# When the expert weights of a graph layer are loaded, and where rows of other experts are masked

## The reference, cut to what matters

```
xn = layernorm(x)                                         # x: 3125 x 256
x  = x + relational_gnn(xn, src, dst, edge_type)          # 50000 edges, 8 relations, 4 bases
       + linear_attention(xn)
xf = layernorm(x)
idx = argmax(xf @ router_w.T + router_b, axis=-1)         # 32 experts, one for each row
h   = relu(xf @ W1[idx] + b1[idx])                        # 256 -> 64
out = relu(h @ W2[idx] + b2[idx])                         # 64 -> 256
x   = x + out
```

## Time and profile before

| | |
|---|---|
| median of 3 runs | 611.94 us (611.05 to 613.35) |
| profiled execution, its own time | 615.56 us |
| its span in the trace | 613.7 us |
| PE, DVE, POOL busy | 86%, 67%, 69% of the span |

### The profile page before, as it was taken

The page is one execution under the profiler, slowest core; times in us unless marked ns, Lnnn a source line. Parts: engine busy times, 40 slices in busy tenths (PEclk is TensorE's granted clock), DMA queues, the critical chain, the costliest instruction groups (busy, mean ns, idle before and its releaser), DMA issues.

```text
span 613.7 us, 10819 instructions
## 1 busy us (share of the span) xinstructions
PE 530.2 (86%) x3165; PEld 445.4 (73%) x3165; DVE 410.6 (67%) x1510; ACT 213.8 (35%) x435; POOL 423.4 (69%) x447
## 2 busy tenths in 40 slices
PE   0656889999968899999999999999996888999880
PEld 0556889999857778888888878888875775776650
DVE  6899587777654647767666676767565870878741
ACT  6685633321107112424243343424240005652300
POOL 6777777777777677777777777777777777334313
PEclk9978899999978699999999999999996658999795
DMA  8994333333354334445454545445448767451101
GB/s 274 266 263 145 104 108 109 104 104 105 110 162 132 99 107 130 141 143 151 138 159 130 154 135 159 141 146 155 135 141 247 216 171 209 134 182 61 45 28 40
DMA packets 47976, 87.17 MB, mean 142 GB/s; under 512 B 11059, under 2 KB 29524, under 8 KB 47784
## 3 DMA queue, kind: packets, MB, share of 16 engines
q0 software_dynamic: 21872, 60.77, 34.1%
q1 hardware_dynamic: 25032, 24.99, 12.9%
q10 hardware_dynamic: 1008, 0.65, 0.4%
HBM read 73.68 MB, written 12.70 MB: 141 GB/s over the span
## 4 chain that ended last, share of the span: by engine, by line
PE 63%; DVE 14%; DMA 7%; POOL 6%; issue 6%; ACT 1%; DVEq 1%; ACTq 0%; POOLq 0%
PE ps L1027 25%; PE ps L1098 12%; PE ps L1081 6%; DMA gath<-xn_d,src_i 6%; POOL gath L682 4%; PE ps L1047 3%; PE ps L1354 3%; PE ps L1069 3%; PE ps L1363 3%; DVE both L2044 2%; POOL acc_raw L682 2%; DVE raw_stats L1501 1%; DMA rel_of<-in_relation_of 1%; PE ps L1323 1%; DVE acc_raw L1590 1%
## 5 line engine op out<-in xcount | busy, mean ns | idle before, releaser
L682 POOL DMA_INDIRECT gath<-xn_d,src_i x263 | 250.6, 953 | 83.4 <-issue 68.6
L1027 PEld LDWEIGHTS ps<-wmat,gath 128*128 128x128 f32 x1052 | 153.3, 213 | 39.3 <-issue 20.6
L1027 PE MATMUL ps<-wmat,gath 128*128 128x80 f32 (+1 forms) x1052 | 161.6, 303 | 15.3 <-DMA gath<-xn_d,src_i 15.1
L682 POOL DMA_INDIRECT acc_raw<-xn_d,src_i x96 | 91.0, 948 | 29.2 <-issue 24.1
L1590 DVE TENSOR_TENSOR acc_raw<-acc_raw,ps 128x144 f32 (+1 forms) x392 | 88.4, 266 | 27.9 <-PE ps L1027 17.9
L1563 DVE TENSOR_TENSOR ps<-rel,iota 128x144 f32<-128x144 f32 (+1 forms) x98 | 28.1, 286 | 92.0 <-PE ps L1027 90.9
L1027 PE MATMUL ps<-wmat,acc_raw 128*128 128x144 f32 x512 | 71.4, 294 | 9.2 <-ACT acc_raw L790 7.8
L1027 PEld LDWEIGHTS ps<-wmat,acc_raw 128*128 128x128 f32 x512 | 68.7, 195 | 12.3 <-issue 8.8
L1567 DVE TENSOR_TENSOR wmat<-ps,wts 128x576 f32<-128x576 f32 (+1 forms) x98 | 62.0, 632 | 3.4
L731 POOL DMA_INDIRECT out<-both,out_i x24 | 24.7, 1030 | 46.2 <-DVE both L2044 22.7
L1098 PE MATMUL ps<-wk_et,acc_raw 128*128 128x256 f32 (+1 forms) x200 | 53.7, 394 | 0.6 <-DVE acc_raw L1590 0.6
(11 more groups left out here) (289 smaller groups left out, 757.2 us busy)
## 6 DMA issues: line engine op xcount, KB each, us to landing
rows_d<-both SPq DMA_DIRECT2D x24, 256.0 KB, 2.5
gath<-xn_d,src_i POOLq DMA_INDIRECT x263, 2.8
both<-in_x SPq DMA_DIRECT2D x24, 128.0 KB, 3.4
both<-in_x SPq DMA_DIRECT2D x4, 640.0 KB, 10.4
xn_d<-both SPq DMA_DIRECT2D x4, 640.0 KB
acc_raw<-in_w_t SPq DMA_DIRECT2D x8, 260.0 KB
acc_raw<-in_w_t SPq DMA_DIRECT2D x8, 256.0 KB
acc_raw<-xn_d,src_i POOLq DMA_INDIRECT x96, 2.8
```

Source lines behind the costliest of these rows:

```text
L682: g.indirect_dma_start(place_of(n), None, table, bass.IndirectOffsetOnAxis(ap=src_i[:, n:n + 1], axis=0)).then_inc(done, 16)
L1027: ins = t_.matmul(ps_edge[quarter][:, m * w:(m + 1) * w], place_of(n)[:, m * P:(m + 1) * P], wmat_tiles[:, k, 0:w], start=k == pair[0], st ...
```

## The change

Weights: expert e's segment of `acc_raw` lies in a quarter of the tiles (e modulo 4). The 16 transfers of weights keep their size, but each takes four experts of one quarter, and it is issued after a row store and an x load of the chain: after tiles 4 to 7, 12 to 15 and 17 to 20 one each, the last four around the stores of tiles 22 and 23. The small transfers follow tile 10. No transfer waits for edge matmuls any more.

Mask: one matmul for each group (bf16, 512 columns) first writes 0 or -3e38 into the PSUM bank of the hidden layer, and the W1 products add to it. ReLU covers 65 rows instead of 64; the 65th has bias 1, so it gives 1 for own rows and 0 for others. DVE builds the mask `never` in `find_pairs` and two small tables in `count_below`. `limit`, the eight memsets of ones and the buffer `picked` go. DVE does a pair in one operation, max with 0 and add to the rows; each waits for the one before.

```diff
-        def load_experts(c):
-            nc.sync.wait_ge(c.pre_done, NS)
...
-            for i in range(PIECES):
-                a, b = X // PIECES * i, X // PIECES * (i + 1)
-                if c is once:
-                    nc.sync.wait_ge(multiplied, OCT * (BRANCH + 1) + OCT // 2 * i)
-                nc.sync.dma_start(segs[:, a:b, 0:P], of_w1[:, a:b, :]).then_inc(ffn_loaded, 16)
-                nc.sync.dma_start(segs[0:H + 1, a:b, W2_AT:W2_AT + D], of_w2[:, a:b, :]).then_inc(ffn_loaded, 16)
+W_LOADS = {**{4 + i: (0, i) for i in range(4)}, **{12 + i: (1, i) for i in range(4)}, **{17 + i: (2, i) for i in range(4)}}
+        def load_piece(eng, quarter, i):
+            half = X // 2 * (i // 2) + quarter
+            of = slice(half, half + X // 2 - 3, 4)
+            if i % 2 == 0:
+                eng.dma_start(segs[:, of, 0:P], of_w1[:, of, :]).then_inc(ffn_loaded, 16)
+            else:
+                eng.dma_start(segs[0:H + 1, of, W2_AT:W2_AT + D], of_w2[:, of, :]).then_inc(ffn_loaded, 16)
...
                 load_x(sp, t + 3, once)
+                if t in W_LOADS:
+                    load_piece(sp, *W_LOADS[t])
+                elif t == SMALL_LOADS:
+                    load_small(sp)
...
+                    bank = ps[5 + g % 2]
+                    t_.matmul(bank[0:H + 1, :], groups[:, g:g + 1].to_broadcast([NPAIR, H + 1]), never.rearrange("p f n -> p (f n)"),
+                              start=True, stop=True)
...
-                            pe.wait_ge(f_read, FT * (g - 2) + f // 2 * 2 + 2)
+                            pe.wait_ge(f_y, FT * (g - 2) + f // 2 * 2 + 2)
...
+                at = o.mark(d.tensor_scalar(member, iota[0:NPAIR, :], facts[0:NPAIR, 2:3], None, ALU.is_ge))
+                at = o.mark(d.scalar_tensor_tensor(member, iota[0:NPAIR, :], facts[0:NPAIR, 3:4], member, ALU.is_lt, ALU.mult))
+                o.mark(d.scalar_tensor_tensor(never, member.unsqueeze(1).to_broadcast([NPAIR, FT, P]), 1.0,
+                                              of_four.unsqueeze(2).to_broadcast([NPAIR, FT, P]), ALU.subtract, ALU.mult))
...
-                        d.tensor_scalar(picked(f), ps[g % 2 * 2 + f // 2][:, f % 2 * D:(f % 2 + 1) * D], limit[:, p:p + 1], 0.0,
-                                        ALU.min, ALU.max).then_inc(f_read, 1)
-                        if f % 2 == 1:
-                            for j in range(2):
-                                place = token_flat[:, ds(tiles[f - 1 + j] * ROW + D, D)]
-                                d.tensor_tensor(place, place, picked(f - 1 + j), ALU.add).then_inc(f_y, 1)
+                        if p > 0:
+                            v.wait_ge(f_y, p)
+                        place = token_flat[:, ds(tiles[f] * ROW + D, D)]
+                        d.scalar_tensor_tensor(place, ps[g % 2 * 2 + f // 2][:, f % 2 * D:(f % 2 + 1) * D], 0.0, place,
+                                               ALU.max, ALU.add).then_inc(f_y, 1)
```

More of the change, by code:

```diff
@@ L442, in gps_layer @@
         at = 0
[L443 to L448, removed]
+        spread = e_flat[:, at:at + 2 * NPAIR].rearrange("p (c j) -> p c j", j=NPAIR)
+        at += 2 * NPAIR
+        never = e_flat[0:NPAIR, at:at + FT * P // 2].bitcast(BF16).rearrange("p (f n) -> p f n", f=FT)
+        at += FT * P // 2
+        member = blank[0:NPAIR, :]
+        of_four = bv_bc[0:NPAIR, 6 * X:6 * X + FT]
+        groups = bv_bc[0:NPAIR, 7 * X:7 * X + NPAIR // FT // 2].bitcast(BF16)
         inv_f = e_flat[:, at:at + NS]
@@ L1353, in hidden @@
                         for k in range(KD):
-                            ins = t_.matmul(ps[5 + g % 2][0:H, f * P:(f + 1) * P], f_w[:, g % 2, f, k * H:(k + 1) * H],
-                                            acc_raw[:, ds(tiles[f] * SEG + XT_AT + k * P, P)], start=k == 0, stop=k == KD - 1)
+                            ins = t_.matmul(bank[0:H, f * P:(f + 1) * P], f_w[:, g % 2, f, k * H:(k + 1) * H],
+                                            acc_raw[:, ds(tiles[f] * SEG + XT_AT + k * P, P)], start=False,
+                                            stop=f == FT - 1 and k == KD - 1, skip_group_check=True)
                     ins.then_inc(f_hid, 1)
@@ L1871, in count_below @@
                 o.mark(d.memset(below[:, 0:1], 0.0))
+                by_four = ident[0:NPAIR, 0:NPAIR].rearrange("p (g f) -> p f g", f=FT)
+                at = o.mark(d.tensor_reduce(of_four, by_four, AX.X, ALU.add))
+                with nc.allow_low_precision("ones and zeros"):
+                    o.mark(d.tensor_reduce(groups, ident[0:NPAIR, 0:NPAIR].rearrange("p (g f) -> p g f", f=FT), AX.X, ALU.add))
+                v.wait_ge(o.sem, at)
+                o.mark(d.tensor_scalar(of_four, of_four, -NEVER, None, ALU.mult))
                 o.mark(d.tensor_tensor_scan(below[:, 1:X + 1], onesb[:, 0:X], oh_sum[:, NS, :], 0.0, ALU.mult, ALU.add))
@@ L1965, in keep_pairs @@
                 v.wait_ge(pairs_done, 1)
[L1966 to L1972, removed]
-                for j in range(2):
-                    for f in range(FT):
-                        at = o.mark(d.memset(f_hts(j, f)[H:H + 1, :], 1.0))
+                known = ps[5][:, 0:2 * NPAIR].rearrange("p (c j) -> p c j", j=NPAIR)
+                o.mark(d.tensor_copy(pair_i[:, :, :], known[0:1, :, :]))
+                o.mark(d.tensor_scalar(last_i[0:1, :], ps[5][0:1, 2 * NPAIR:2 * NPAIR + NS], 1.0, None, ALU.max))
+                at = o.mark(d.memset(segs[H:H + 1, 0, B_AT:B_AT + X], 1.0))
                 v.wait_ge(o.sem, at)
@@ L2083, in _ @@
                 v.wait_ge(once.pre_done, NS)
+                v.wait_ge(ffn_loaded, 16 * EARLY_LOADS)
                 for j in range(3):
```

51 lines of the change are left out of this document (29 added, 22 removed).

## The result

| | before | changed |
|---|---|---|
| median of 15 runs | 612.72 us | 607.79 us |
| lowest to highest | 610.65 to 617.92 | 606.48 to 609.19 |
| ratio, with 95% interval | 1 | 0.991 (0.9885 to 0.9934) |
| profiled execution: span, its time | 613.7, 615.56 us | 606.5, 608.28 us |

The ratio is 5.5 us less (4.0 to 7.0); the medians lie 4.9 apart. Three runs in the rounds of the experiments stood far above the others (649, 699 and 1310 us); the medians hold them, the ratios leave them out. The two profiled executions lie 7.3 us apart, since that of before stood 3 us above its median. I split these 7.3 at three instants of PE and POOL: the first turn of sorted tiles (the expert stage begins), the W1 products of group 13 and the last scatter. The late octets and all ahead of them gave 3.5 (511.07 to 507.56), the expert stage 2.4 (80.08 to 77.71 us), the end 1.3 (13.06 to 11.74 us).

A forecast was written before the change was run, and what follows sets the result against it. PE and POOL were taken to bound the chain, weight transfers to hold the late octets, PE with late DVE the expert stage. Terms -2.75 + 1.0 - 3.1 - 0.9 = -5.75 gave 606.2 us, range 601.0 to 611.0.

The forecast's parts named there:

- part 1: Late octets: without the burst of weight transfers, ranking and the short tile's product start earlier, -2.75 us.
- groups 0 to 7: Expert stage, first eight groups: PE is the bound, gains only a 0.74 stall, pays new matmuls: +1.0 us.
- groups 8 to 13: Expert stage, last six groups: PE's 2.72 us wait for DVE and the clock's fall go, new matmuls cost +1.3: -3.1 us.
- the end: Last scatters behind the short tile's sum: four pairs on DVE get shorter, -0.9 us.
- The early transfers: Chain of tiles: twelve weight transfers cost nothing, covered by half-idle DMA engines and eight gather buffers.
- Part 2: Expert stage: one more mask matmul per group costs PE 0.22 us, +3.1 for 14 groups.
- Part 3: DVE in expert stage and end: one operation makes a pair 0.66 us, saving 0.9 per group.
- Part 4: Small edits, mask tables and `never` on DVE: covered by edge matmuls and gathers, so 0; +2 us if both covers are gone.
- A: Rival: full clock holds through the late octets, so the short tile's product takes half: 602.1 us, chance 0.16.
- B: Rival: POOL's rhythm holds late octets to 0.98 gain, the 2.72 wait shrinks by only 1.8: 610.5 us, chance 0.20.
- C: Rival: weight transfers in the chain hold up gathers, 1.1 us each, 13 in all: 619 us, chance 0.10.

The follow-up runs named there:

- added matmuls: Changed kernel plus bf16 matmuls of 512 columns in the late octets, whose results nobody reads: 606.10 us, 0.9880 of the kernel before.
- the 66th row: Changed kernel with mask matmuls replaced by one more row of W2 and the hidden layer, brought by small transfers: 602.61 us, 0.9828 of before.
- fewer added matmuls: Changed kernel with mask as one more W2 row and three unread matmuls per late quarter, none behind the last: 600.92 us, 0.9807 of before.

## Why the prediction was right, and where by chance

**Sum.** -5.75 was forecast and -5.5 measured (-4.9 by the medians); against the profiled execution 609.8 was forecast and its time is 608.28. Of the terms, between profiled executions: part 1 -2.75 forecast, -3.5 seen; groups 0 to 7 +1.0 and +0.9 (first turn to `first_layer`: 40.03 to 40.89 us); groups 8 to 13 -3.1 and -3.2 (40.05 to 36.82); the end -0.9 and -1.3.

**Part 1** held in its mechanism: the hole at 463 went, ranking moved by 3.2, DVE's sequence carried the lead on. The run that did it alone has 1.8 by its time and the pair of profiles 3.5, which also holds 0.4 of an earlier start, as the last chain step of the short tile shows, before and changed:

```profile
455.52 1.92 PE L1081 MATMUL ps<-cmat,both 128*53 128x512 f32 x4
455.12 1.92 PE L1098 MATMUL ps<-cmat,both 128*53 128x512 f32 x4
```

From this step to the first turn it is 55.55 us in the trace of before and 55.05 in that of the mask and the single operation alone, the two with the weights behind the chain. It is 51.56 to 53.65, 52.44 in the middle, in the seven with early weights and no added matmuls. That is 2.9 less, so the 2.75 was right in size.

**The early transfers** cost nothing, and doubled they cost nothing. The Trainium skill, "DMA: Bandwidth & Descriptors", section "Issuing engines are not separate DMA queues", says that all transfers share the 16 engines. In the chain, where the share rose from 0.48 to 0.54 and 0.59, no run here shows a price for that; at 0.98, in the earlier trace rows, one was seen.

**Part 2 was mis-sized**: the step "at the full clock half of it, 0.21, so I take 0.22". The 0.21 is right for the columns, but the step left out what stands between this matmul and the next operation's. It measured 0.32, and 14 make 4.4, not 3.1. That the stage came out near its forecast all the same (-2.4 against -2.1) is luck, since two other terms were too small, on the other side. PE's idle time fell by 4.3 us (6.75 to 2.44, table below), where 0.74 and 2.72 were counted. And the slow stretch behind the wait, counted at 1.7 for the W1 products alone, gave some 2.4: from the matmul of 576.72 to `finish_last` it was 6.82 us, and from that of 572.65 it is 4.68, with a mask matmul in it. `finish_last` before, and now:

```profile
583.54 3.66 PE L1323 MATMUL ps<-gath,wts 128*53 128x256 f32 x16
577.33 3.66 PE L1340 MATMUL ps<-gath,wts 128*53 128x256 f32 x16
```

**Part 3 had the right size, and its cause was only half right.** Two edits could each remove the wait of 2.72 or most of it: DVE earlier by the single operation, or PE later by the mask matmul. The step said that DVE comes 3.6 earlier and PE 0.9 later, and that therefore the wait goes. The four kernels that have the one, the other, both or neither show the stage from first turn to group 13:

| stage, us (PE idle in it) | without mask matmul | with it |
|---|---|---|
| two DVE operations | 80.08 (6.75), before | 78.67 (3.31) |
| one DVE operation | 73.27 (2.61) | 77.71 (2.44), changed |

PE's idle time is the stage less PE's busy time, from windows over it. The kernel without any mask does less than the others, but that with the 66th row, which masks, has the same stage, 73.26, and waits of the same 2.6 us. Of before, the last of five stretches of the stage and the sum of all five:

```profile
575.07:591.15 16.08, 14.43 (x62) 9.40 (x62) 8.64 (x22) 1.34 (x5) 3.47 (x4) 0.79 0.10 34
sum 80.08, PE 73.33 PEld 53.07 DVE 51.96 ACT 33.81 POOL 33.66; mean PE 14.67 PEld 10.61 DVE 10.39 ACT 6.76 POOL 6.73
```

The last stretch of the run with two DVE operations:

```profile
569.83:584.50 14.67, 14.35 (x71) 8.89 (x70) 8.47 (x23) 3.19 (x13) 4.85 (x5) 1.00 0.13 46
```

And that of the changed kernel:

```profile
571.56:585.27 13.71, 13.71 (x70) 8.38 (x68) 4.41 (x10) 2.62 (x11) 4.85 (x5) 1.00 0.14 49
```

The mean clock was 0.79 in before's and is 1.00 in both others. Alone, the single operation would give 6.8 us in the stage, and the mask matmul even makes it 1.4 shorter where DVE has two operations, since PE's idle time falls by 3.4 us and the clock stays up, which together outweigh 14 x 0.32 us of work. Together they share one wait. So the gain that the single operation could bring was mostly spent on the matmul that made it possible, and the 66th row, which does without that matmul, brings it back.

**Part 4.** The 0 holds within what can be seen: ranking starts near its forecast of 477.6, and the run with mask and single operation alone, which has these edits beside late weights, takes 55.05 us from the last chain step of the short tile to the first turn, against 55.55 before. (The edits count six DVE operations, three of them in `find_pairs`, where the step says seven.) They were not tried by themselves.

**Rivals.** A did not come: the clock was 0.50 from 488 to 500. Where it was made to hold, it gave some 2.5 us and not 4.1, so its 602.1 was too low as well: the product took 3.6 and not half of 6.2, and it let the edges' time count, which POOL's rhythm covers. The Trainium skill, "TensorE: Matmul & The Clock Gate", section "HAM oscillation — how this bites in real kernels", has it that waits for DMA make the clock fall. The trace of the changed kernel agrees, with waits for DVE beside those for DMA: the clock is 1.00 from 480 to 484, then PE waits 0.6 us for a gather and 1.5 for a table and is busy for 1.40 of 4 us until 488, and behind that the clock is 0.50. B did not come: the late octets gave 2.9 and not 0.98, and the wait at `spread_hidden` went whole, with the full clock behind it. C is excluded by the doubled transfers.

## What to carry to other kernels

Where two edits remove the same wait, price each alone and both: their gains don't add, and the one that costs work may only be filling time that the other frees. A small matmul between others costs its columns and the way to the next operation; read the price from start to start, in the kernel. A mask can ride as one more row of a contraction that is computed anyway, at no cost on PE, if transfers that nobody waits for can bring it.

## What the runs showed of the hardware

The 0.11 us between the mask matmul and W1 is no general price of going from bf16 to float32. In the run with added matmuls four of them and the start of the float32 edges behind are 0.87 us apart (489.30 to 490.17), which is four times 0.21 and 0.03. Here the weight load of the first W1 product starts late, with nothing named as its releaser:

```profile
509.92 0.74 PEld L1374 LDWEIGHTS ps<-acc_raw,cmat 128*64 128x64 f32 x7 [0.23 <-issue]
```

W1's products take addresses from registers and the edges don't, but that can't be all of it: in `spread_hidden`, whose addresses are fixed, the float32 matmul starts 0.27 behind a bf16 one of 424 columns (572.84 to 573.11), and that one 0.19 behind its twin (572.65 to 572.84). The cause was not tried and stays open.

From 488 to 500 the clock stayed at 0.50 in the changed kernel with PE busy for 11.02 of 12 us, and at 0.50 with 11.35 of 12 in the run with two DVE operations. With fewer added matmuls between the edges it was 1.00:

```profile
488.00:500.00 12.00, 10.98 (x85) 7.91 (x85) 10.88 (x60) 0.00 (x0) 8.95 (x11) 1.00 0.40 112
```

So the busy time of the stretch does not tell the two levels apart. Nor is it a matter of edge matmuls as such: in the changed kernel PE is busy for 8.00 of 8 us from 468 to 476, mostly with edge matmuls of 128x80, and the clock is 0.50 throughout; in the kernel before, 24 edge matmuls of 128x144 ran from 183.90 on without a wait, and the clock rose from 0.50 to 1.00 between 189 and 190. What makes the difference was not taken apart.
